# Preparation stage of a hybrid attention, mixture and recurrence kernel: the gate's inner product from the mixed rows, and another order of each batch's jobs

## What is computed

```python
shifted = concatenate([zeros_like(hidden_states[:, :1]), hidden_states[:, :-1]], axis=1)
delta = shifted - hidden_states              # hidden_states: layer-normed rows
xr = hidden_states + delta * x_r             # and xw, xk, xv, xa in the same way
r = xr @ W_r
log_w = -softplus(-(tanh(xw @ w_lora_a) @ w_lora_b + w_lora_bias)) - 0.5
k = xk @ W_k;  v = xv @ W_v
a = sigmoid(xa @ a_lora_a @ a_lora_b + a_lora_bias)
g = sigmoid(r @ g_lora_a) @ g_lora_b + g_lora_bias
kk = (k * k_k) per head, divided by its norm
k = k * (1.0 + (a - 1.0) * k_a)
bonus = ((rh * kh * r_k).sum(-1, keepdims=True) * vh)
```

## Time and profile before

| | |
|---|---|
| median of 3 runs | 4448.77 us (4448.08 to 4449.37) |
| the profiled execution's own time | 4428.87 us |
| its span | 4427.2 us |
| PE busy | 3939.1 us (89%) |
| DVE busy | 3213.9 us (73%) |
| ACT busy | 2185.7 us (49%) |
| POOL busy | 2048.9 us (46%) |

### The profile page before, as it was taken

One profiled execution on the slowest core, in us unless ns is written; L12 is line 12 of the kernel. 1 busy time (PEld: TensorE's weight loads), 2 busy tenths in 40 slices (PEclk: granted clock), 3 DMA queues, 4 the chain that ended last, 5 costly groups with the idle time before them and its releaser, 6 DMA issues. The chain is left out here.

```text
span 4427.2 us, 72079 instructions
## 1 busy us (share of the span) xinstructions
PE 3939.1 (89%) x23448; PEld 2688.4 (61%) x23448; DVE 3213.9 (73%) x8707; ACT 2185.7 (49%) x7361; POOL 2048.9 (46%) x1668
## 2 busy tenths in 40 slices
PE   5999999999996696988849999999999999957598
PEld 2344444444445464666637888888888888846466
DVE  5777777777756111799859999999999999958310
ACT  1666666666666211444413555655555555624211
POOL 2211211221213421122238888888888888824422
PEclk7999999999997798999979999999999999977799
DMA  4323322332346232244342232322323223157232
GB/s 111 80 76 73 99 74 75 87 83 58 92 102 199 92 129 85 105 171 171 152 100 33 35 43 35 41 36 36 42 35 42 35 37 40 21 153 248 86 129 80
DMA packets 479034, 378.41 MB, mean 85 GB/s; under 512 B 298378, under 2 KB 440997, under 8 KB 472544
## 3 DMA queue, kind: packets, MB, share of 16 engines
q1 hardware_dynamic: 466400, 348.90, 32.4%
q0 software_dynamic: 12288, 25.28, 1.7%
HBM read 222.13 MB, written 159.58 MB: 86 GB/s over the span
## 5 line engine op out<-in xcount | busy, mean ns | idle before, releaser
L750 DVE TENSOR_REDUCE at_neg_max<-at_slot 128x1 f32<-128x512 f32 (+3 forms) x1216 | 745.6, 654 | 247.9 <-PE at_slot L542 245.0
L672 ACT ACTIVATE at_prob<-at_slot 128x512 f32<-128x512 f32 (+1 forms) x1216 | 631.1, 577 | 355.2 <-PE at_slot L562 354.4
L2157 PE MATMUL sc_added<-sc_outer,sc_ident 128*128 128x128 f32 x4096 | 586.3, 286 | 78.6 <-POOL sc_outer L1908 57.7
L2157 PEld LDWEIGHTS sc_added<-sc_outer,sc_ident 128*128 128x128 f32 x4096 | 496.9, 192 | 209.3 <-DVE sc_state L2058 115.2
L1921 POOL TENSOR_TENSOR sc_terms<-sc_seen,sc_pack 128x1024 f32<-128x1024 f32 (+2 forms) x288 | 605.1, 2143 | 13.7 <-PE sc_ps_o L2179 13.7
L2179 PE MATMUL sc_ps_o<-sc_terms,sc_ident 128*128 128x256 f32 x2048 | 608.6, 381 | 2.1 <-POOL sc_terms L1921 2.1
L390 POOL TENSOR_SCALAR_AFFINE_SELECT at_prob<-at_prob 128x512 f32<-128x512 f32 x256 | 162.8, 636 | 888.6 <-ACT at_prob L672 888.4
L2081 ACT ACTIVATE sc_seen<-sc_state 128x512 f32<-128x512 f32 x256 | 152.8, 597 | 756.0 <-DVE sc_decayed L2022 748.3
L542 PE MATMUL at_slot<-at_k_stack,at_q_stack 96*128 96x512 bf16 (+3 forms) x1536 | 459.7, 335 | 22.3 <-DMA at_k_stack<-parts 19.9
L1908 POOL TENSOR_TENSOR sc_outer<-sc_pack 128x2048 f32<-128x2048 f32 x128 | 467.3, 3671 | 5.0
L562 PE MATMUL at_slot<-at_q_stack,at_k_stack 99*128 99x512 bf16 (+3 forms) x1536 | 453.1, 331 | 12.2 <-ACT at_prob L672 11.8
(11 more groups left out here) (306 smaller groups left out, 7128.3 us busy)
## 6 DMA issues: line engine op xcount, KB each, us to landing
packed<-pr_pack SPq DMA_DIRECT2D x16, 3072.0 KB, 13.4
sc_pack<-packed SPq DMA_DIRECT2D x512, 96.0 KB, 3.7
parts<-at_parts SPq DMA_DIRECT2D x96, 256.0 KB
f_up_w<-in_ffn_wi SPq DMA_DIRECT2D x16, 1024.0 KB, 5.1
f_down_w<-in_ffn_wo SPq DMA_DIRECT2D x16, 1024.0 KB, 8.9
at_q_stack<-parts SPq DMA_DIRECT2D x32, 384.0 KB
at_k_stack<-parts SPq DMA_DIRECT2D x32, 384.0 KB
slots<-at_no_row SPq DMA_DIRECT2D x2, 4128.0 KB
```

The source lines that it names most:

```text
L672: act.activation(prob[:, first:first + n, q1 - tiles * P:q1], ps[:, 0:n * tiles * P].rearrange("p (n k) -> p n k", n=n), ACT.Exp)\
L750: dve.tensor_reduce(neg_max[:, chunk, qt, h:h + n], ps[:, 0:n * tiles * P].rearrange("p (n k) -> p n k", n=n), AX.X, ALU.max, negate=True) ...
L2157: pe.matmul(added[h][:, 0:HALF], ident[:], outer[m % 2][:, 2 * n + s, h * HALF:(h + 1) * HALF], start=(s == 0), stop=False)
```

## The change

- **Gate.** Since r = xr W_r, the product r g_lora_a is xr (W_r g_lora_a). The matrix `r_to_g` is made once, ahead of the first batch, by the new jobs `turn_w` and `fold`; `g_inner` is made from `mixed["r"]`. `turn_r` is gone, with its 16 transposes and 2 copies a batch.
- **Biases of w and a** are a 65th row of `inner_b`, against a row of ones in `inner`: DVE's two additions for each are gone, and ACT takes the sigmoid straight from PSUM.
- **Normed rows** are made by ACT (`affine`), from `shift` = -mean/std; DVE makes only `shift` (8 columns).
- **Key.** ACT copies k into the field FK; DVE reads `kk` and FK from there instead of from PSUM.
- **Bonus.** The second instruction of each half of `bonus` goes from DVE to POOL; DVE keeps the sum, as job `dots`.
- **Order.** The halves no longer stand side by side. The slots go on round from batch to batch. The eight turns are written out, without a loop.
- **Stores.** SP loads the next `x` first, and stores each half as gate, pack, bonus.

```diff
-    return [("normalise", 0), ("turn_x", 0), ("turn_x", 1), ("mix", "r"), ("mix", "w")]
+    return [("stats", 0), ("root", 0), ("affine", 0), ("turn_x", 0), ("turn_x", 1), ("turn_w", 0), ("fold", 0),
+            ("mix", "r"), ("mix", "w"), ("mix", "a")]
...
-    return (halves("r") + halves("turn_r") + [("w_inner", 0), ("g_inner", 0), ("mix", "a")]
-            + plus([("normalise", 0)]) + halves("w") + [("mix", "v"), ("a_inner", 0)] + halves("g") + halves("a") + [("mix", "k")]
-            + plus(halves("turn_x")) + halves("v") + plus([("mix", "r")]) + halves("k")
-            + halves("key") + plus([("mix", "w")]) + halves("bonus"))
+    jobs = [("r", 0), ("w_inner", 0), ("mix", "v"), ("mix", "k"), ("a_inner", 0), ("g_inner", 0), ("w", 0), ("a", 0),
+            ("+stats", 0), ("v", 0), ("+root", 0), ("k", 0), ("+affine", 0), ("g", 0), ("key", 0), ("+mix", "r"),
+            ("r", 1), ("+turn_x", 0), ("+turn_x", 1), ("w", 1), ("dots", 0), ("v", 1), ("+mix", "w"), ("g", 1),
+            ("bonus", 0), ("a", 1), ("k", 1), ("+mix", "a"), ("key", 1), ("dots", 1), ("bonus", 1)]
...
+        ring = tuple((sum(used[-1]) + n) % PREPARE_SLOTS for n in range(PREPARE_SLOTS))
+        plans.append(Plan(jobs, PREPARE_USER, dict.fromkeys(("act", "dve"), ring)))
...
-            with eng.Fori(0, BATCH - 1) as b:
-                part(turn_counts(turn, b), b, b + 1)
+            for b in range(BATCH):
+                part(turn_counts(b), b, b + 1 if b + 1 < BATCH else None)
...
+                    elif stage == "bonus":
+                        pool.wait_ge(dots_ready, 1 + b * 2 + what + 1)
+                        slots.wait_read(pool, ("v", what))
+                        pool.wait_ge(bonus_stored[what], 1 + b * 16)
+                        pool.tensor_tensor(by_head(bonus[what][:]), field(what, FV),
+                                           dots[what][:].unsqueeze(2).broadcast_to([P, HALF_TILES * HEADS, D]),
+                                           ALU.mult).then_inc(bonus_ready, 1)
...
+                    elif stage == "turn_w":
+                        pe.wait_ge(loaded, 1 + 16 * N_LOADS)
+                        for n in range(KC):
+                            for k in range(KC):
+                                last = pe.transpose(ps[:, n * C + k * P:n * C + (k + 1) * P],
+                                                    big["r"][:, k, n * P:(n + 1) * P], ident[:])
+                    elif stage == "fold":
+                        slots.wait_read(pe, ("turn_w", 0))
+                        for k in range(KC):
+                            for n in range(KC):
+                                last = pe.matmul(ps[:, k * RG:(k + 1) * RG], big_r_turned[:, n, k * P:(k + 1) * P],
+                                                 inner_a["g"][:, n, :], start=(n == 0), stop=(n == KC - 1))
...
+                    elif stage == "affine":
+                        act.wait_ge(affine_ready, 1 + f + 1)
+                        for n in range(TILES):
+                            act.activation(xn[:, n, :], x[:, n, :], ACT.Identity, bias=shift[:, n:n + 1],
+                                           scale=rstd[:, n:n + 1]).then_inc(xn_ready, 1)
...
+                        dve.wait_ge(xn_ready, 1 + f * TILES)
                         in_start.link(dve.reciprocal(rstd[:], std[:]))
-                        for t in range(TILES):
-                            dve.tensor_scalar(xn[:, t, :], x[:, t, :], mean_var[:, t, 0:1], rstd[:, t:t + 1],
-                                              ALU.subtract, ALU.mult).then_inc(xn_ready, 1)
+                        dve.scalar_tensor_tensor(out=shift[:], in0=rstd[:], scalar=-1.0, in1=mean_var[:, :, 0],
+                                                 op0=ALU.mult, op1=ALU.mult).then_inc(affine_ready, 1)
```

More of the change, by code:

```diff
@@ L2259, in prepare @@
         rstd = sb("rstd", [P, TILES])
+        shift = sb("shift", [P, TILES])
         turned = sb("turned", [P, KC, T + 1])
@@ L2345, in store @@
             def store(slots, b, next_x):
+                if next_x is not None:
+                    load_x(next_x)
                 for h in range(2):
@@ L2350, in store @@
                                  gate_sb[h][:].rearrange("p (n c) -> p n c", c=C)).then_inc(gate_stored[h], 16)
-                if next_x is not None:
-                    load_x(next_x)
-                for h in range(2):
-                    rows = bass.ds(b * TILES + h * HALF_TILES, HALF_TILES)
+                    slots.wait_read(sp, ("v", h), alone=True)
+                    sp.wait_ge(chain, 1 + b * TURN + 5 * (h + 1))
+                    sp.nop(nofuse=True)
+                    for packed_field in (w_packed, r_packed, key_ready):
+                        sp.wait_ge(packed_field, 1 + b * 2 + h + 1)
+                        sp.nop(nofuse=True)
+                    sp.dma_start(packed[rows].rearrange("n p f -> p n f"),
+                                 pack[h][:].rearrange("p (n h) f -> p n (h f)", h=HEADS)).then_inc(pack_stored[h], 16)
                     sp.wait_ge(bonus_ready, 1 + b * 2 + h + 1)
@@ L2369, in _ @@
             load_x(1)
-            with sp.Fori(0, BATCH - 2) as b:
-                store(turn_counts(turn, b), b, b + 2)
-            store(turn_counts(turn, BATCH - 2), BATCH - 2, None)
-            store(turn_counts(last_turn, BATCH - 1), BATCH - 1, None)
+            for b in range(BATCH):
+                store(turn_counts(b), b, b + 2 if b + 2 < BATCH else None)
             for h in range(2):
@@ L2381, in _ @@
             own.up(pool.memset(turned[:], 0.0))
+            own.done()
+            for m in "wa":
+                own.link(pool.memset(inner[m][RW:RW + 1, :], 1.0))
             own.link(pool.memset(ident[:], 0.0))
@@ L2460, in part @@
                 if b is None:
-                    pe.wait_ge(loaded, 1 + 16 * N_LOADS)
+                    slots.wait_read(pe, ("fold", 0))
             run(pe, part)
@@ L2492, in part @@
                         act.activation(field(what, FV), by_head(ps[:]), ACT.Copy).then_inc(emptied[s], 1)
-                    elif stage == "turn_r":
-                        act.activation(r_turned[:, what, :], ps[:], ACT.Copy).then_inc(emptied[s], 1)
+                    elif stage == "k":
+                        act.activation(field(what, FK), by_head(ps[:]), ACT.Copy).then_inc(emptied[s], 1)
+                    elif stage == "turn_w":
+                        act.activation(big_r_turned[:].rearrange("p n c -> p (n c)"), ps[:, 0:KC * C], ACT.Copy)\
+                           .then_inc(emptied[s], 1)
+                    elif stage == "fold":
+                        act.activation(r_to_g[:].rearrange("p k g -> p (k g)"), ps[:, 0:KC * RG], ACT.Copy)\
+                           .then_inc(emptied[s], 1)
                     elif stage in ("w_inner", "a_inner", "g_inner"):
```

134 lines of the change are left out of this document (56 added, 78 removed).

## The result

The changed kernel takes 4381.22 us in the median of 4 runs (4375.22 to 4389.97), the kernel before 4448.43 (4447.17 to 4449.37, 4 runs). The ratio is 0.9854, with a 95% interval of 0.9841 to 0.9866: 65 us less by the ratio and 67 by the medians, where 55 were predicted, and inside the range given. The profiled execution is the slowest of the four: its own time is 4389.97, its span 4388.2 us.

The account below looks back on a forecast made before the run. DVE's work and waits were taken to bound each preparation turn. Six turns of 6.2, plus 3, 7 and 11, less 1.6, gave 56.6, taken as 55: 4448.8 - 55 = 4394 us, range 4366 to 4424.

Parts of the forecast that it names:

- the ring of a turn runs through DVE: 51.9 busy and 6.5 idle: Preparation stage before the change: what leaves DVE shortens the 58.4 us turn until PE is full.
- Turn 58.4 to 52.2: Each of six preparation turns would fall from 58.4 to 52.2 us, gaining 6.2.
- The layout: New turn laid out instruction by instruction from the end of key 1: 52.3 us; work 38.4, port waits 10.5, idle 2.9.
- So the bonus product earns nothing: Moving the bonus product to POOL: DVE gives 2.45 and gets 4.8 of port waits, a loss of 2.3 us a turn.
- Last turn, -7: From r of the last turn to the end of FB: 68.4 us would become about 61.
- First turn and start, -3 and +1.6: Turn 1 would fall from 49.9 to about 46.5 us, 3 gained; r of turn 1 would come 1.6 later.
- The end, -11: From the last FB to the recurrence's first load: 25.5 us would become 14.2, with half 0 stored in mid turn.
- unless a store took over 28 us: Pack stores issued at 29 and 52.4 land at 42 and 66, before ACT needs the places at 62 and 80.
- Straight code, 0: Extra instruction fetching for the written-out turns: taken as 0, at most 0.5 us a turn.
- the port costs less: Rival, chance 0.05: POOL and DVE overlap in most new places, PE bounds the turn at 46 to 47, time 4349.
- PE's clock falls: Rival, chance 0.04: more but shorter waits hold PE at half clock; with 20 us so, turn 62 and time 4470.
- the gain may go to waits not seen: Rival, chance 0.04: DVE's freed time, 6 us a turn, goes to unseen waits at mix v or the gate; nothing gained.

Follow-up runs that it names:

- old_fold: The kernel before with only the gate's matrix folded, its order, loop, biases and stores kept: 4448.1 us against 4449.0 on the same chip, turn 58.4.
- port: Changed kernel with POOL's r 1 product after mix r, both bonus products after dots 1, half 1's gate earlier, bonus stores last: 4322.8 us, turn 44.9.
- pool_quarter: Changed kernel with POOL's six products of a turn cut to a quarter of their columns: 4317.8 us, turn 44.5.
- stores_last: Changed kernel with the stores in the old order, both bonuses and both pack halves at the turn's end: 4404.2 us, turn 55.8.
- halves: Changed kernel's operations, stores and slots, but with both halves of each job side by side in the order: 4467.1 us, turn 61.5.
- bonus_on_dve: Changed kernel with the bonus product moved back from POOL to DVE, behind each dots: 4378.3 us, turn 53.0.
- late_r1: Changed kernel in which POOL's product of r 1 waits for mix r: 4363.5 us, turn 50.8.
- port_root: The kernel port with the root of the next batch's statistics ahead of the copies of v 0 on ACT: 4328.1 us, turn 46.0.

## Why the prediction was right, and where it was not

**The bound of the kernel before, "the ring of a turn runs through DVE: 51.9 busy and 6.5 idle".** Wrong, or half the ring. I had read six turns as one. By single turns, before, two of the six are 3.3 us longer than the others with the same busy time of DVE (windows):

```profile
1820.14:1880.73 60.59, 51.31 (x202) 37.74 (x200) 51.91 (x65) 28.18 (x30) 11.30 (x4) 0.89 0.42 156
1938.02:1995.32 57.30, 48.38 (x201) 35.33 (x200) 51.92 (x65) 28.09 (x30) 11.31 (x4) 0.94 0.44 165
```

and the timeline of PE shows where: in the long turn the products of a and the transposes of `xn` run at a lower clock (granted 0.62 over the two groups, 1.00 in the short turn),

```profile
1858.16 5.28 PE L2457 MATMUL pr_slot<-pr_a_inner_b,pr_a_inner 64*128 64x256 f32 x16 [1.13 <-ACT pr_a_inner L2498]
1863.37 3.67 PE L2424 MATMUL pr_slot<-pr_ident,pr_xn 128*128 128x128 f32 x16
...
1976.05 3.72 PE L2457 MATMUL pr_slot<-pr_a_inner_b,pr_a_inner 64*128 64x256 f32 x16 [1.13 <-ACT pr_a_inner L2498]
1979.70 1.97 PE L2424 MATMUL pr_slot<-pr_ident,pr_xn 128*128 128x128 f32 x16
```

5.28 + 3.67 against 3.72 + 1.97 is 3.3 us, and the turn is longer by all of it. So from the a products through v and k to `scaled` the ring ran on PE; DVE's wait for k, 1.7 in most turns and 3.4 in two, was the sign of it. Of DVE's work only what stands outside that piece shortens a turn, which fits the bias rows: of the 4.6 that they took from DVE, 1.9 came back as a longer wait for k (3.6 for 1.7), and the other 2.7 are the 2.6 by which the turn fell below the shorter ones of before. That `turn_r` was off the ring, as predicted, is shown by `old_fold`.

**Turn 58.4 to 52.2.** Measured 51.16. The layout's terms: work 38.4, measured 38.6; port waits 10.5, measured 8.7; idle 2.9, measured 3.9. The port was mis-sized by the bonus product: 2.38, the length of a product in the recurrence, was taken for it, and it is 1.93 (1.9 in `port`, where two take 3.81), below even the bound of 2.3, so `mix v` and `mix w` wait 1.7 each instead of 2.4; `mix k` waits 2.1 instead of 2.3 and the clamps 1.4 instead of 1.6. The idle was mis-sized at the root, 2.0 instead of 0.4, and at the gate, 0.3 instead of 1.2. Both belong to one stretch, the one beside PE's 10.75 us, in which only its sum counts. The layout had PE's v, k and gate half in 10.3 from `mix v`; v 0 runs at a lower clock for part of its length and takes 1.8 more, but the wait for `mix k` that I had ahead of k did not arise. The places of the port waits were all four right. That the turn came out within 1.0 us is in part luck: the port waits were 1.8 too dear and the idle time 1.0 too cheap, and in PE's stretch a lost clock of 1.8 took the place of a wait of 1.3 that did not come. What carried the forecast is the layout, which had PE's stretch in it, and not the sentence on the bound.

**"So the bonus product earns nothing".** Wrong, with its price of a loss of 2.3 us a turn. Undone, it costs 1.85 a turn. The step that failed is the account "DVE gives 2.45 and gets 4.8": it counts DVE's time wherever it lies. The product on POOL costs 3.4 of port waits on the ring, 1.7 in `mix w` and 1.7 in `mix v`, not 4.8. The product on DVE costs its 2.45 there, and besides it POOL's product of r 0 then holds `mix v`, on the ring, for the 2.1 that it took from `mix k`, beside the ring. The Trainium skill, GPSIMD Engine Reference, section Engine selection, prefers VectorE for an elementwise product, GpSimd being about twice as slow with two inputs; here VectorE is the faster too, 1.22 to 1.93 for the bonus product (1.6 times) and 2.36 for `rr` (1.9 times), but moving the product to VectorE makes the changed kernel slower. The Trainium skill, GPSIMD Engine Reference, section Key points, says that the two engines contend for SBUF when VectorE reads two inputs there or runs in a 2-port mode; the waits in the mixes and in FA agree with the first. The clamp has one input, and no run here shows which mode it runs in. `pool_quarter` and `port` put 6.3 to 6.7 us a turn on the port waits and the lower clock behind them.

**Last turn, -7.** Measured -9.4; no experiment was made on it. **First turn and start, -3 and +1.6.** -2.3 and +1.9. **The end, -11.** -11.4, and `stores_last` shows its cause. That the pack stores are hidden, "unless a store took over 28 us", when they are "issued at 29 and 52.4" was right too, and mattered more than the text said. **Straight code, 0:** no sign of it; 3.2 of DVE's 3.9 us of idle time a turn and 5.2 of PE's 5.3 are waits with other names.

**The rivals.** That the port costs less was right in its sign only, 8.7 for 10.5, and by a shorter product, not by an overlap of the two engines. That PE's clock falls did not come: 0.97 against 0.91 over the six turns. It does fall in one place, after PE's wait of 2.6 for `mix v` (granted 0.67 over v 0, and 1.00 over what follows it), and costs 1.8 us there, on the ring. That the gain may go to waits not seen: not here, but `halves` is that case.

**What stays open:** how the 6.3 us a turn between the changed kernel and `port` divide. The port waits taken out of DVE's part sum to 5.2, v 0 at full clock is 1.8, and PE's own bound cuts the sum short; no kernel changed the one without the other. How the 7.2 us a turn between the kernel before and the changed one divide among ACT's normed rows, k by way of `pack`, the order, the slots going round and the straight code: no run has one of them alone, and `halves` sets one particular table against the new order. And why every second turn of `bonus_on_dve` and some turns of `late_r1` and `port_root` are longer.

## What to carry to other kernels

Before pricing work that leaves an engine, cut the turn at the two or three handovers and see which engine is waited for in each piece: time saved counts only in the piece where that engine is the one waited for, and where one turn is longer than its neighbours, the engine whose delay it follows is on the ring. A second engine's product that shares the port should stand beside a stretch in which the first one waits anyway; here a choice of places, with the same instructions, was worth another 43 us. Alternating halves keeps two engines busy at once, but needs its buffers free earlier, so look at the stores of the turn before as well.

## What was not expected of the hardware

- POOL's product of 128 x 1024 float32 takes 2.36 us with two full inputs (`rr`) and 1.90 to 1.93 where the second is 64 columns broadcast over 16 (`bonus`).
- Products of a quarter of that size, 128 x 256, took 0.73 us (`rr` by the key) where the port was free. The others of `pool_quarter` show 1.6 to 1.7 in the mean, among port waits of both engines that I did not take apart.
- In every pair shown here, DVE and POOL took turns by whole instructions, also when one is small: a clamp of 64 columns takes 0.19 us in `pool_quarter`, and in the changed kernel, beside POOL's product, 0.87 in the mean and 1.04 at 2006.46, where it ends with that product (2007.5).
